# Moving the writes of Q's and K's bf16 parts from SyncE's DMA queue to ScalarE's, with both stack loads in a row on SyncE's

## The reference

```
qkv = hidden_states @ w_attn + b_attn
q, k, v = jnp.split(qkv, 3, axis=-1)
scores = jnp.einsum('bqhd,bkhd->bhqk', q, k) * SCALE
scores = jnp.where(causal, scores + slopes * rel, -jnp.inf)
attn = softmax(scores);  out = einsum(attn, v) @ w_proj + b_proj
```

## Time and profile before

| | us |
|---|---|
| median of 3 runs | 936.98 (936.16 to 938.35) |
| the profiled execution's own time | 934.45 |
| its span, first to last instruction | 932.7 |
| PE busy / DVE busy / ACT busy / POOL busy in it | 863.8 / 758.7 / 437.7 / 264.1 |
| Q and K pass: first matmul of piece 0 to first of V | 334.87 to 402.65 |

### The profile page before, as it was taken

The page is one execution under the profiler, slowest core; times in us unless marked ns, Lnnn a source line. Parts: engine busy times, 40 slices in busy tenths (PEclk is TensorE's granted clock), DMA queues, the critical chain, the costliest instruction groups (busy, mean ns, idle before and its releaser), DMA issues.

```text
span 932.7 us, 12157 instructions
## 1 busy us (share of the span) xinstructions
PE 863.8 (93%) x4217; PEld 413.1 (44%) x4223; DVE 758.7 (81%) x1622; ACT 437.7 (47%) x798; POOL 264.1 (28%) x214
## 2 busy tenths in 40 slices
PE   5988878899979999899999999999999999999996
PEld 3434424354427454344444444444434444444442
DVE  5679999999997974699899989997245799776876
ACT  4667654656652032100666666667542656433100
POOL 1048898899994100040000000000000334000000
PEclk8879988999999999999999999999999999999999
DMA  9200060300006016610443144400014000000001
GB/s 349 94 0 1 1 270 0 136 1 0 1 0 202 1 57 152 176 63 5 83 79 66 20 72 79 71 10 3 1 64 179 0 1 0 0 1 0 12 34 45
DMA packets 21127, 54.33 MB, mean 58 GB/s; under 512 B 4949, under 2 KB 11733, under 8 KB 18058
## 3 DMA queue, kind: packets, MB, share of 16 engines
q1 hardware_dynamic: 21066, 53.56, 20.4%
HBM read 44.96 MB, written 8.39 MB: 57 GB/s over the span
## 4 chain that ended last, share of the span: by engine, by line
PE 61%; DVE 6%; DMA 2%; POOL 1%; ACT 1%; issue 1%; SPq 0%; POOLq 0%; DVEq 0%
PE ps L1182 16%; PE ps L1044 7%; PE ps L1193 6%; PE ps L1026 6%; PE ps L1066 4%; PE ps L1013 3%; PE ps L1010 3%; PE ps L1103 3%; PE ps L955 3%; PE ps L1083 3%; DMA parts_dram<-qkp 2%; PE ps L1029 2%; DVE ps L1450 1%; PE ps L768 1%; PE ps L949 1%; PE ps L958 1%
## 5 line engine op out<-in xcount | busy, mean ns | idle before, releaser
L721 ACT ACTIVATE prob<-ps 128x512 f32<-128x512 f32 x288 | 160.0, 599 | 126.0 <-PE ps L1029 97.7
L468 POOL TENSOR_TENSOR hC<-hs,C_sb 128x512 f32<-128x512 f32 x128 | 162.3, 1283 | 58.8 <-ACT C_sb L659 32.2
L933 PE MATMUL ps<-hC,identf 128*128 128x512 f32 x256 | 139.7, 652 | 22.9 <-POOL hC L468 22.2
L1026 PE MATMUL ps<-stack 123*128 123x512 bf16 (+3 forms) x384 | 113.8, 327 | 0.2
L592 ACT ACTIVATE ps<-dtT,nA 128x512 f32<-128x512 f32 x128 | 88.1, 689 | 50.0 <-DVE hs L1335 46.6
L424 POOL TENSOR_TENSOR rstd<-veps,mhalf 128x4 f32<-128x4 f32 x8 | 8.5, 1067 | 353.4 <-DVE veps L1220 353.4
L1457 DVE TENSOR_REDUCE mrow<-ps 128x1 f32<-128x512 f32 x128 | 81.9, 684 | 10.0 <-PE ps L1013 9.7
L933 PEld LDWEIGHTS ps<-hC,identf 128*128 128x128 f32 x256 | 46.3, 200 | 89.9 <-POOL hC L468 71.6
L1044 PE MATMUL ps<-prob,V 128*32 128x512 f32 (+3 forms) x768 | 81.6, 498 | 0.7 <-ACT prob L721 0.7
L1313 DVE TENSOR_TENSOR dBx<-uT,ps 128x512 f32<-128x512 f32 x112 | 74.1, 663 | 7.2 <-PE ps L833 6.2
L1182 PE MATMUL ps<-hT,wg 128*128 128x512 f32 (+1 forms) x176 | 79.1, 592 | 0.0
(11 more groups left out here) (199 smaller groups left out, 1334.6 us busy)
## 6 DMA issues: line engine op xcount, KB each, us to landing
wmod<-in_wmod SPq DMA_DIRECT2D x4, 1536.0 KB, 11.3
parts_dram<-qkp SPq DMA_DIRECT2D x16, 384.0 KB, 2.6
stack<-parts_dram SPq DMA_DIRECT2D x16, 384.0 KB
wmod<-in_wmod SPq DMA_DIRECT2D x4, 1024.0 KB, 10.6
stack<-parts_dram SPq DMA_DIRECT2D x16, 256.0 KB
wattn<-in_wattn SPq DMA_DIRECT2D x1, 3072.0 KB, 11.3
wg<-in_wg SPq DMA_DIRECT2D x1, 2752.0 KB, 11.4
wu<-in_wu SPq DMA_DIRECT2D x1, 2752.0 KB, 9.3
```

What stands on the lines that cost most here:

```text
L468: pool.tensor_tensor(hC[:, c, :], hs[:, c, :], C_sb[:, m % 2, :], ALU.mult).then_inc(S["hc_done"], 1)
L721: A_(prob[:, u % 4, j, :], ps[:, 3 + F % 3, :], ACT.Exp).then_inc(S["exp_done"], 1)
L933: mm(ps[:, c, :], identf[:], hC[:, c, :], start=False, stop=(s == NS - 1), skip_group_check=True).then_inc(S["sum_done"], 1)
L1026: ins = mm(ps[:, bank, col:col + w], qk[0:ATT_ALL, 1, j, tile(kb)], qk[0:ATT_ALL, 0, j, q0:q0 + w], start=True, stop=not diag)
```

## The change

SP's loop over the 16 pieces goes. ACT issues the write of piece i-1 right after its copy of piece i, after waiting for that piece's split, and the write of piece 15 at the end. SP waits for the writes of pieces 0 to 4 and then issues the loads of stack 0 and stack 1 one behind the other.

```
-            for i, (ob, h) in enumerate(QK_ORDER):
-                sp.wait_ge(S["qk_split"], i + 1)
-                sp.dma_start(parts_dram[:, ob * P:(ob + 1) * P, half(h)].rearrange("q p t -> p q t"), qkp[:, i % 3, :, :]) \
-                  .then_inc(qk_wr[i % 3], 16)
-                if i == 4:
-                    for r in range(3):
-                        sp.wait_ge(qk_wr[r], 16 * (2 if r < 2 else 1))
-                    load_stack(0)
-                if i == 6:
-                    load_stack(1)
+            for r in range(3):
+                sp.wait_ge(qk_wr[r], 16 * (2 if r < 2 else 1))
+            load_stack(0)
+            load_stack(1)
             for i in range(3):
                 sp.wait_ge(qk_wr[i], 16 * len(range(i, 16, 3)))
@@ in the program of ScalarE
+            def write_parts(i):
+                ob, h = QK_ORDER[i]
+                act.wait_ge(S["qk_split"], i + 1)
+                act.dma_start(parts_dram[:, ob * P:(ob + 1) * P, half(h)].rearrange("q p t -> p q t"), qkp[:, i % 3, :, :]) \
+                   .then_inc(qk_wr[i % 3], 16)
             for i in range(16):
                 if i == QK_FIRST:
                     ln_out(2, 1, 0, 1, (1,))
                 ...
                 A_(qkf[:, i % 2, :], ps[:, qk_bank(i), :], ACT.Identity, ...)
+                if i:
+                    write_parts(i - 1)
+            write_parts(15)
```

## The result

The changed kernel took 946.10 us (median of 4 runs, 943.62 to 947.09), the kernel before 937.66 us (median of 4, 936.16 to 939.38). The ratio is 1.009, interval 1.0068 to 1.0112: slower by 8.4 us, against a forecast of 9.4 and a predicted time of 946.4. The profiled execution has a span of 941.8 us, 9.1 more than before. Of these 1.8 stand ahead of the Q and K pass, where nothing was changed. The start of that pass lay between 334.9 and 338.3 us over the eleven profiles of this study, so that part is scatter. From the first V matmul to the end the two profiles take the same (530.1 before, 530.0 after). What grew is the pass itself, from piece 0 to V: 402.65 - 334.87 = 67.8 before and 411.85 - 336.68 = 75.2 after, 7.4 us more.

The account below looks back on a forecast made before the run. TensorE was taken to set the pace of the Q and K pass. Later stack loads, slow writes and the clock put V at 412.05, not 402.65: +9.4 us on the median 936.98 gives 946.4, 8-in-10 range 934.0 to 949.0.

Parts of the forecast that it names:

- The mechanism: Writes on ACT's queue beside stack loads on SP's: engines take one packet of either queue in turn; 946.4 us, chance 0.5.
- 24 x 0.85 us: Write 5 beside the stack loads: its 24 small packets each wait for a large one, landing 22 us after issue.
- Which write is late: Before splits 8 and 9: write 5 lands at 384.8, 22 us after issue, and write 6 follows at 388.4.
- Part 4: Writes beside loads on two queues: TensorE stops 10 us, the clock costs 1.2 us, V starts 9.4 us later.
- Part 1: Write of piece 0 ahead of hT's second half: TensorE waits 1.4 us before piece 3, all later pieces shift by that.
- Part 2: Stack 0's loads wait for write 4, now issued behind copy 5: 2.4 us later, loads start at about 362.2.
- Part 3: Stack 0 takes 13.2 us from first issue to first score as today; there at 375.4, TensorE waits 3 us.
- rival 2: Queues share fairly by bytes or bundles; writes land in 5 to 7 us, stack 0 comes later: 937.3 us, chance 0.17.
- What can be won: First scores to V: TensorE's waits for mask and row maximum and a slow piece, 1.84 + 2.82 + 1.19 = 5.85 us.
- Rivals 1 to 3: Writes beside loads: untouched, 934.3 us (0.25); fair share, 937.3 (0.17); only a 2.5 us delay of V, 939.5 (0.08).
- rival 1: Writes pass beside the loads as if alone, landing in 2.6 us, and DVE is never late: 934.3 us, chance 0.25.

## Why the prediction was right, and where its steps were not

- **The mechanism** was the forecast's for the second part of write 6's time: packets of the two queues take turns one for one. It is shown by the counts by queue with rows of 8 and 4 KB, 284 to 315, 380 to 368 and 242 to 240, and, less cleanly, by what 4 KB rows gave back, 8.1 us of the pass. On the Trainium skill (DMA: Bandwidth & Descriptors, Queues, rings and completion order): the turn by packets agrees with it, but here a packet was a single 1 KB row, not the 9 to 17 descriptors it calls typical.
- **The 20.5 us of write 6 agree with the 20 to 22 forecast by luck.** The forecast was 24 turns of 0.8 + 0.05 us, 20.4, from the moment of issue. Write 6 stood still for the first 6.4 us or so (367.64 to 374), a term that the forecast did not have, and then shared for 14.1. A turn was shorter than forecast: from the shares of the stretch 375 to 384 us I estimate 0.40 us for a packet of SyncE's queue and 0.10 for one of ScalarE's, 0.50 in all and 12 us for 24 turns, since a third of SyncE's packets were small and an 8 KB row took 0.6 us and not 0.8.
- **Which write is late** was wrong. The term 24 x 0.85 us was laid on write 5 (22 us). Write 5 landed within 7.6 us; write 6 took the 20.5. The step assumed that turns start as soon as both queues have work. With only one write late and not two in a row, split 9 began at 388.2, which is 386.4 on the clock of before, against 388.4 forecast.
- **Part 4's wait and clock.** I forecast a stop of 10 us and 1.2 us for the clock. It was 6.05 us and 2.63 + 1.39 = 4.0 us, because the clock fell already behind the 3.14 us wait, so that piece 10 ran slow and filled part of the stop. The restart at piece 11 came at 391.22 - 1.81 = 389.4, forecast 391.25. From there to V it took 20.6 us, forecast 20.8. So the 2 us by which the pass grew less than forecast (7.4, not 9.4) lie ahead of piece 11. That 946.4 stands so near 946.10 is in part luck too: the forecast added 9.4 to a median of 936.98, which a fourth run moved to 937.66, and the measured difference is 8.4.
- **Part 1** (1.4 forecast, 1.28 measured) was right as a wait. As a term of the pass it was too large: taking it away won 0.5 us of the pass. The medians can't settle it for the time.
- **Part 2** was too pessimistic. ScalarE issues a DMA as the ACTIVATE ahead of it starts, not as it ends (360.77 and 360.78). The first stack load came 26.7 us after piece 0, forecast 27.3, before 24.8.
- **Part 3.** Stack 0 took 377.67 - 363.42 = 14.3 us and not 13.2. Write 5's bytes may have gone in front of part of it, as in my rival 2, but this is not shown: with both stacks in a row on one queue and no write beside them stack 0 took 13.8.
- **What can be won** (5.85 us from the earlier trace rows) was real: 4.6 us of the pass came back by moving stack 1 alone, 6.3 with the mask.
- **Rivals 1 to 3** fall: no write passed stack 1 untouched, and DVE's long wait stayed. Even with no second stack in flight write 6 took 10.3 us and not the 2.6 of rival 1.

What stays open: why a write in ScalarE's queue first stands still and then goes in a burst while SyncE is still issuing. In the profile after, write 5's and write 6's packets began only after some of the stack packets had been taken, about those of the loads issued ahead of each write. The same was seen with 4 KB rows, where write 6 (issued at 368.96) got 5 packets from 369 to 371 us and had landed by 375.7. That order of issue counts across the two queues is my reading; no run isolates it, and it leaves open how much of the gain of 4 KB rows is packet size and how much the slower issue.

## What to carry to other kernels

A second DMA queue is no fast lane. A small transfer on it can still take as long as all that the other queue has in flight, because in these runs the queues shared by packets and not by bytes (0.32 MB against 1.58 in the same 9 us), so the one with small rows loses. Before moving a transfer to another engine's queue, ask what large transfer need not be in flight at that time: here a load wanted only some 60 us later cost 4.6 us of the pass on one queue, and moving it was a one-line edit. And when a DMA is put into a compute engine's program, look at what its wait stands in front of.

## What the runs showed of the hardware that I had not expected

- A write issued from ScalarE starts together with the ACTIVATE ahead of it in the program (360.78 and 360.77), and its 0.37 us of issue delayed no copy behind it: the copies kept their 3.43 us from one to the next, with 2.75 us of idle time to hide it in.
- TensorE's waits for stack 0 of 1.71 to 2.33 us left the clock of piece 10 alone, and those of 2.56 to 3.40 us slowed it, but not in the order of their lengths: piece 10 lost 1.2 us behind 2.56, 2.7 behind 2.82 (4 KB rows), 1.7 behind 2.86, 2.6 behind 3.14 and 1.7 behind 3.40.
- Loads of the same bytes in 16-partition pieces brought stack 0 later: 17.5 us from the first issue to the first score, against 13.2 before and 14.3 in the change.
